# GpSimd's long elementwise operations issued in pieces of 256 elements a partition

## The chip, the cores and the metric

The kernel runs on one core of one Trainium2 chip. The metric is the device time of one execution, in microseconds (us). The kernel before takes 765.38 us, the median of 3 runs. The core's engines are TensorE (PE in the profile; PEld is its weight load), VectorE (DVE), ScalarE (ACT), GpSimd (POOL) and SyncE (SP, which issues most DMAs). Each works through its own instructions in order, and they meet at semaphores.

## The reference

Two transformer layers over x of 8 batches x 256 tokens x 256 channels, in float32. In each layer the attention and the feed-forward part read the same normalised input:

```python
xn = _layernorm(x)
x = x + _L0_attn_ref(xn, ...) + _L0_ffn_ref(xn, ...)
xn = _layernorm(x)
x = x + _L1_attn_ref(xn, ...) + _L1_ffn_ref(xn, ...)
```

- Layer 0 attention: 16 heads of 16 channels, causal, with a bias that is linear in the distance; the softmax's result is held to at least 1e-10.
- Layer 0 feed-forward: 8 experts, each `silu(xn @ Wg) * (xn @ Wu) @ Wd` with 256 hidden channels. All experts are computed, and their outputs are summed with routing weights.
- Layer 1 attention: 16 heads, causal, plain softmax.
- Layer 1 feed-forward: two linear layers (256 to 1024 to 256) with ternary weights, `alpha * sign(W) * (|W| > 0.05 max|W|)`, where alpha is the mean of the kept |W|; a gelu between them; and last a quantisation of the result to 4 bits with one scale for the whole tensor.

## The kernel before

**Numbers in two parts.** Most matmuls run on float16 pairs: a float32 tile is split into a high part (its float16 rounding) and a low part (the rest), and three products are summed (high by high, low by high, high by low). ScalarE makes the high part, and VectorE or GpSimd the low part by a subtraction. The weights of layer 0 (query/key, gate/up, down) are split once in the first pass: 14 tiles of 128 x 1024, of which GpSimd has the low parts of six (`POOL_SPLITS`, line 869) and VectorE the others. They come in through two alternating raw buffers, and the load of tile i + 2 waits until the low part of tile i is done.

**Experts.** For each batch and expert, TensorE makes `gate` and `up` (L1162), ScalarE a tanh and VectorE two operations that give the hidden tile `hid0` (128 x 512 float32). ScalarE writes its high part `h0_hi` (L1018), GpSimd its low part `h0_lo` (L880), and TensorE's `down` (L1173) needs both. Layer 1's hidden tile is eight blocks of 256; ScalarE writes the high parts of two blocks at a time (L1032), and GpSimd the low parts (L903).

**Ternary weights.** In the first pass, for W1 and then W2 (128 x 2048 float32 each): VectorE finds the largest |w|, and writes a tile of -1, 0 and 1. GpSimd multiplies the weights by it in place (L918), which leaves |w| where it is kept. ScalarE then makes two sums, of the kept |w| and of the squared signs (L958, L960). TensorE transposes the sums (step `tsm`, L1119) and VectorE makes alpha from them. Before its loop TensorE waits for both alphas (`pe.wait_ge(s_t, 2 * TERN)`).

**Attention.** For each head of layer 0: TensorE makes scores, VectorE adds the bias and takes the row maximum (L1555), ScalarE the exponential (L1037), VectorE the reciprocal of the sum (L1577) and the normalisation of the probabilities (L1580: one instruction of 256 and one of 128 elements, from SBUF to SBUF). TensorE then transposes them (L1233 to L1235). In layer 1 VectorE takes the maxima (L1569), and GpSimd masks the exponentials of the diagonal blocks (L889) before TensorE uses them (L1280).

**Order.** Batches are software pipelined: layer 1 of a batch runs beside layer 0 of the next. There are four kinds of pass: `first`, `steady` (a loop over 6 iterations), `last` and `final`. The order of the steps on each engine is written out by hand in `ORDER_TEXT`, once for each engine and kind. GpSimd's order in the loop is

```python
ln1a up up:1 h1 up:2 h1:2 h1:1 h1:3 up:3 up:4 mp +ln0a s:3 s mp:1 up:5 s:4 s:2 up:6 s:1 s:7 s:5
+xe s:6 up:7
```

where `up` is L880, `h1` L903, `s` L889, `ln0a` and `ln1a` the residual with its bias (L844) and the inverse deviation (L850). Nothing plans at run time: an engine that comes to a wait stands there.

Of the kernel before, what the change touches and what calls it, by code (L numbers as in the profile page):

```python
# [33 lines left out]
ALU = mybir.AluOpType  # L34
# [4 lines left out]
B, S, D = 8, 256, 256  # L39
H, C = 16, 16  # L40
NT = S // P
NK = D // P
E, F = 8, 256
NF = F // P
HID = 1024
# [300 lines left out]
def wait(eng, sem, value):  # L346

    if not (isinstance(value, int) and value <= 0):
        eng.wait_ge(sem, value)
# [21 lines left out]
def two_blocks(nc, x, wqk0, bqk0, wv0, vb0, wo0, ob0, slopes, wg, wu, wd, temp,  # L371
               wqk1, bqk1, wv1, vb1, wo1, ob1, w1t, b1c, w2t, b2, out):
    with ExitStack() as ctx:
        def sb(name, shape, dt=F32):
            return ctx.enter_context(nc.sbuf_tensor(name, shape, dt))

        def sem(name):
            return ctx.enter_context(nc.semaphore(name))
# [68 lines left out]
        hid0 = sb("hid0", [P, 2, NF, S])  # L447
        h0_hi = sb("h0_hi", [P, 2, NF, S], F16)
        h0_lo = sb("h0_lo", [P, 2, NF, S], F16)
        hid1 = sb("hid1", [P, NH, S])  # L450
        h1_parts = sb("h1_parts", [P, 2, NH, S], F16)
# [29 lines left out]
        raw = [v_sb[1][:].rearrange("p t b c -> p (t b c)")[:, 0:2 * NK * D], yx_sb[:].rearrange("p a t d -> p (a t d)")]  # L481
# [41 lines left out]
        s_lop = sem("s_lop")  # L523
        s_t = sem("s_t")
        s_tu = sem("s_tu")
# [27 lines left out]
        s_h0l = sem("s_h0l")  # L553
# [3 lines left out]
        s_h1l = sem("s_h1l")  # L557
# [37 lines left out]
        def split_parts(i):  # L595

            what, a = SPLIT[i]
            if what == "qk":
                return [w[a][:].rearrange("p k n -> p (k n)") for w in (qk_hi, qk_lo)]
            if what == "gu":  # L600
                return [w[:, a].rearrange("p m k f -> p (m k f)") for w in (gu_hi, gu_lo)]
            return [w[:, a:a + 2].rearrange("p e k d -> p (e k d)") for w in (wd_hi, wd_lo)]

        def his_done(i):
            return i + 1 + sum(k <= i for k in POOL_SPLITS)
# [6 lines left out]
        def tern_of(i):  # L612
            return ((w1_raw, t1_sb[:].rearrange("p k n -> p (k n)")), (w2_raw, t2_sb[:].rearrange("p a d -> p (a d)")))[i]
# [168 lines left out]
        def _(pool):  # L782
# [20 lines left out]
            def tables():  # L803

                pool.memset(ones[:], 0.0).then_inc(s_tab, 1)
                pool.memset(pieces[:], 0.0).then_inc(s_tab, 1)
                pool.memset(pick[:], 0.0).then_inc(s_tab, 1)
                pool.tensor_copy(ident_b[:], ident[:]).then_inc(s_tab, 1)
                pool.wait_ge(s_tab, 3)
                pool.memset(ones[:, C:2 * C], WSCALE).then_inc(s_tab, 1)  # L810

                for i, row in enumerate((0, 4, KR, KR + 4)):
                    if i:
                        pool.wait_ge(s_tab, 5 + i)
                    pool.affine_select(out=pick[:], in_=pick[:], compare_op=ALU.not_equal, fill=1.0, base=-row,
                                       pattern=[[-1, 4], [0, P]], channel_multiplier=1).then_inc(s_tab, 1)
# [13 lines left out]
            def do(st):  # L830
# [35 lines left out]
                if name == "split" and st.arg in POOL_SPLITS:  # L866
                    hi, lo = split_parts(st.arg)
                    pool.wait_ge(s_hi, his_done(st.arg))
                    pool.tensor_tensor(lo, raw[st.arg % 2], hi, ALU.subtract).then_inc(s_lop, 1)
                if name == "xe":  # L870
                    wait(pool, s_xl[0], n.at(1, 1))
                    wait(pool, s_h0, n.at(E))
# [4 lines left out]
                if name == "up":  # L877
                    e = st.arg % 2
                    wait(pool, s_h0h, n.at(E, st.arg + 1))
                    pool.tensor_tensor(h0_lo[:, e], hid0[:, e], h0_hi[:, e], ALU.subtract).then_inc(s_h0l, 1)  # L880
                if name == "s":
                    for hp in range(2):
                        s = 2 * st.arg + hp
# [16 lines left out]
                if name == "h1":  # L900
                    a = 2 * st.arg
                    wait(pool, s_h1h, n.at(NH // 2, st.arg + 1))
                    pool.tensor_tensor(h1_parts[:, 1, a:a + 2], hid1[:, a:a + 2], h1_parts[:, 0, a:a + 2],  # L903
                                       ALU.subtract).then_inc(s_h1l, 1)
                if name == "quant":
                    c = st.arg

# [6 lines left out]
                if name == "tern":  # L914
                    i, step = st.arg // TERN_STEPS, st.arg % TERN_STEPS
                    if step == 3:
                        pool.wait_ge(s_t, TERN * i + 6)
                        pool.tensor_tensor(tern_of(i)[0], tern_of(i)[0], tern_of(i)[1], ALU.mult).then_inc(s_tu, 1)  # L918
                    if i == 0 and step == 0:
                        tables()  # L920
                    if i == 1 and step == 5:
                        pool.wait_ge(s_lo, len(SPLIT) - len(POOL_SPLITS))
                        pool.wait_ge(s_lop, len(POOL_SPLITS))
                        pool.wait_ge(s_hi, his_done(len(SPLIT) - 1))
                        pool.memset(v_sb[1][:], 0.0).then_inc(s_v1z, 1)

            def before_block1():
                pool.sem_inc(s_h1l, NH // 2)
                pool.sem_inc(s_mp, 4)
                pool.sem_inc(s_mk, H)  # L930

            run_passes(nc, pool, do, before_block1, "gpsimd")


# [739 lines left out]
```

## Time and profile before

| | us |
|---|---|
| median of 3 runs | 765.38 (764.9 to 766.98) |
| the profiled execution | 762.38 |
| its span, first to last instruction | 760.6 |
| TensorE busy | 644.9 (85%), 6455 matmuls |
| VectorE busy | 570.8 (75%) |
| ScalarE busy | 465.4 (61%) |
| GpSimd busy | 270.1 (36%), 386 instructions |
| mean granted TensorE clock | 0.958 of full |

Durations below are from this one profiled execution. Busy time is what an engine spends in instructions, a wait not counted; it doesn't say which engine sets the end. For that there is the chain that ended last, which is followed back from the last instruction through whatever released each step. An instruction's duration on VectorE or GpSimd can contain time in which it stood, so the same shape with two durations is worth a look.

### The profile page before, as it was taken

How to read it: one execution, taken by the hardware profiler on the slowest of the kernel's cores; microseconds unless marked ns; L12 is line 12 of the kernel's file. 1: busy time of each engine (PE TensorE's matmuls, PEld its weight loads, DVE VectorE, ACT ScalarE, POOL GpSimd, SP SyncE). 2: the span in 40 equal slices, each digit the busy share in tenths (PEclk: the TensorE clock that was granted, in tenths of full speed). 3: DMA queues.
4: the chain of work that ended last, by engine and by line, in shares of the span. 5: the costliest groups of instructions: out<-in, count | busy, mean ns of one | idle time of the engine just before them, and what ended most of it. 6: DMA issues, size and time to landing. Idle time of an engine off the chain costs nothing.

```text
span 760.6 us, 19948 instructions
## 1 busy us (share of the span) xinstructions
PE 644.9 (85%) x6455; PEld 480.6 (63%) x6455; DVE 570.8 (75%) x2203; ACT 465.4 (61%) x1223; POOL 270.1 (36%) x386
## 2 busy tenths in 40 slices
PE   1476676989989997999889997999899997999773
PEld 0354554767666775777666775777676775767542
DVE  4489867796687948796779858796779768886557
ACT  2567765954379454965389445965398435963652
POOL 7846541224404241142404241233313331135336
PEclk9989998999999999999999999999999998999996
DMA  6843021300303030302212030302211030300453
GB/s 203 273 127 117 8 77 49 97 17 16 124 14 110 14 110 28 109 1 69 83 35 76 14 110 28 110 4 68 80 58 53 14 110 16 112 3 1 153 181 110
DMA packets 49555, 56.72 MB, mean 75 GB/s; under 512 B 5104, under 2 KB 40048, under 8 KB 49520
## 3 DMA queue, kind: packets, MB, share of 16 engines
q1 hardware_dynamic: 46480, 52.44, 21.6%
q0 software_dynamic: 1056, 2.62, 1.0%
q10 hardware_dynamic: 1984, 1.21, 0.5%
q8 instruction: 19, 0.31, 0.2%
q14 instruction: 16, 0.13, 0.1%
HBM read 33.71 MB, written 22.54 MB: 74 GB/s over the span
## 4 chain that ended last, share of the span: by engine, by line
PE 58%; DVE 16%; ACT 11%; issue 8%; POOL 2%; DMA 2%; ACTq 1%; SPq 1%; DVEq 1%; POOLq 0%
PE gen_ps L1162 16%; PE gen_ps L1173 9%; PE gen_ps L1135 6%; PE value_ps L1280 5%; PE gen_ps L1193 4%; PE gen_ps L1210 3%; ACT hid L1025 3%; PE value_ps L1286 3%; PE score_ps L1223 2%; ACT probs L1037 2%; DVE probs L1555 2%; DVE inv L1591 2%; DVE probs L1580 2%; PE turn_ps L1249 2%; PE turn_ps L1233 2%
## 5 line engine op out<-in xcount | busy, mean ns | idle before, releaser
L880 POOL TENSOR_TENSOR h_lo<-hid,h_hi 128x512 f16<-128x512 f32 x64 | 74.4, 1163 | 271.6 <-ACT h_hi L1018 271.6
L1037 ACT ACTIVATE probs<-probs,nmax 128x256 f32<-128x256 f32 (+1 forms) x256 | 113.4, 446 | 29.0 <-DVE nmax L1555 28.6
L1162 PE MATMUL gen_ps<-xe_hi,gu_hi 128*128 128x256 f16 x512 | 101.0, 280 | 2.1 <-issue 2.1
L1162 PE MATMUL gen_ps<-xe_lo,gu_hi 128*128 128x256 f16 x512 | 100.6, 279 | 0.0
L1162 PE MATMUL gen_ps<-xe_hi,gu_lo 128*128 128x256 f16 x512 | 100.4, 279 | 0.0
L1555 DVE CUSTOM_DVE_ANT_0 probs<-score_ps,bias 128x256 f32<-128x256 f32 (+1 forms) x256 | 79.1, 351 | 16.5 <-PE score_ps L1225 16.5
L1065 ACT ACTIVATE et<-turn_ps 128x384 f32<-128x384 f32 x124 | 54.0, 489 | 50.9 <-PE turn_ps L1255 48.6
L1569 DVE CUSTOM_DVE_ANT_0 junk<-score_ps,bias 128x256 bf16<-128x256 f32 x248 | 73.6, 353 | 14.2 <-PE score_ps L1225 13.3
L1580 DVE TENSOR_SCALAR probs<-probs,rsum 128x256 f32<-128x256 f32 (+1 forms) x256 | 76.5, 341 | 4.6
L1014 ACT ACTIVATE tanh_sb<-gen_ps 128x512 f32<-128x512 f32 x64 | 37.8, 591 | 64.6 <-PE gen_ps L1162 64.5
L889 POOL TENSOR_SCALAR_AFFINE_SELECT et<-et 128x256 f32<-128x256 f32 x128 | 51.3, 423 | 73.0 <-ACT et L1065 73.0
L1223 PE MATMUL score_ps<-k_stack,q_stack 64*128 64x256 f16 x252 | 36.3, 285 | 44.0 <-DVE nmax L1555 26.0
L1046 ACT ACTIVATE pt<-turn_ps 128x384 f32<-128x384 f32 x128 | 60.4, 482 | 20.3 <-PE turn_ps L1235 20.2
L1173 PE MATMUL gen_ps<-wd_hi,h_hi 128*128 128x256 f16 x256 | 50.1, 278 | 9.7 <-issue 6.8
L1223 PEld LDWEIGHTS score_ps<-k_stack,q_stack 64*128 64x128 f16 x252 | 12.2, 93 | 72.2 <-DVE nmax L1555 30.7
L1162 PEld LDWEIGHTS gen_ps<-xe_hi,gu_hi 128*128 128x128 f16 x512 | 47.7, 100 | 14.3 <-issue 8.4
L1162 PEld LDWEIGHTS gen_ps<-xe_lo,gu_hi 128*128 128x128 f16 x512 | 51.3, 100 | 7.0
L1513 DVE SCALAR_TENSOR_TENSOR acc<-gen_ps,w,acc 128x256 f32<-128x256 f32 x112 | 48.8, 477 | 9.2 <-PE gen_ps L1173 9.2
L1162 PEld LDWEIGHTS gen_ps<-xe_hi,gu_lo 128*128 128x128 f16 x512 | 51.2, 100 | 6.9
L1502 DVE SCALAR_TENSOR_TENSOR hid<-gated,gen_ps 128x512 f32<-128x512 f32 x64 | 43.8, 684 | 11.4 <-PE gen_ps L1162 10.7
L903 POOL TENSOR_TENSOR h_parts<-hid,h_parts 128x512 f16<-128x512 f32 x32 | 37.3, 1178 | 38.4 <-ACT h_parts L1032 38.4
L1497 DVE SCALAR_TENSOR_TENSOR gated<-tanh_sb,gen_ps 128x512 f32<-128x512 f32 x64 | 43.6, 682 | 9.7 <-ACT tanh_sb L1014 9.7
(225 smaller groups left out, 1662.7 us busy)
## 6 DMA issues: line engine op xcount, KB each, us to landing
scr_q<-parts SPq DMA_DIRECT2D x32, 256.0 KB, 2.7
scr_k<-parts SPq DMA_DIRECT2D x32, 256.0 KB, 3.0
q_stack<-scr_q SPq DMA_DIRECT2D x64, 128.0 KB, 3.0
k_stack<-scr_k SPq DMA_DIRECT2D x64, 128.0 KB, 3.1
x<-in_x SPq DMA_DIRECT2D x8, 256.0 KB, 2.7
y_dram<-yx_sb SPq DMA_DIRECT2D x7, 256.0 KB, 2.2
x_dram<-yx_sb SPq DMA_DIRECT2D x7, 256.0 KB, 2.2
out_dram<-gu_hi SPq DMA_DIRECT2D x7, 256.0 KB, 2.2
```

The costliest lines, as they stand in the source:

```text
L880: pool.tensor_tensor(h0_lo[:, e], hid0[:, e], h0_hi[:, e], ALU.subtract).then_inc(s_h0l, 1)
L889: pool.affine_select(out=on_diagonal, in_=on_diagonal, compare_op=ALU.is_ge, fill=0.0, base=0, pattern=[[0, NT], [1, P]], channel_multipli ...
L1037: last = act.activation(probs[:, k, lo:hi], probs[:, k, lo:hi], ACT.Exp, scale=-1.0, bias=nmax[:, k, j:j + 1], accum_out=esum[:, k, j:j + 1])
L1046: act.activation(pt[:, slot:slot + 3].rearrange("p t q -> p (t q)"), turn_ps[s % 2][:, 0:3 * P], ACT.Copy).then_inc(s_ev[0], 1)
L1065: act.activation(et[:, s % TURNED], pair_of(st)[hp][:, 0:3 * P], ACT.Exp).then_inc(s_ev[1], 1)
L1162: last = pe.matmul(g[:, S * f:S * f + S], w[:, st.arg, m, k, cols], xx[:, k, :], start=(i == 0), stop=(i == len(terms) - 1))
L1173: last = pe.matmul(g[:, D * t:D * t + D], h[:, st.arg % 2, f, P * t:P * t + P], w[:, st.arg, f, :], start=(i == 0), stop=(i == len(terms) ...
L1223: pe.matmul(pair[hp][:, 0:S], q[rows[hp], i, P:S], k[rows[hp], i, :], start=True, stop=True)
L1513: dve.scalar_tensor_tensor(acc[:, t], g[:, D * t:D * t + D], w8[:, t, e:e + 1], (xb[0] if st.place == 0 else acc)[:, t], ALU.mult, ALU.add)\
L1555: last = dve.tensor_tensor_reduce(out=probs[:, k, lo:hi], in0=g[:, lo:hi], in1=bias0[:, s, blo:S], scale=-1.0, scalar=BIG, op0=ALU.add, op ...
L1569: last = dve.tensor_tensor_reduce(out=junk[:, hp, lo:hi], in0=pair_of(st)[hp][:, lo:hi], in1=bias1[:, blo:S], scale=-1.0, scalar=BIG, op0= ...
L1580: last = dve.tensor_scalar(probs[:, k, lo:hi], probs[:, k, lo:hi], rsum[:, k, j:j + 1], CLAMP, ALU.mult, ALU.max)
```

## The change

Each of four kinds of GpSimd operation is issued as a row of instructions over 256 elements a partition, and the last one of them raises the semaphore that the one instruction raised before. The low parts of a weight tile (1024 elements) become four, those of a hidden tile (512, both layers) two, and a ternary product (2048) eight. Operands, types and the order of the steps stay as they were, and no other operation is touched.

```diff
--- before.py
+++ after.py
@@ -866,7 +866,9 @@
                 if name == "split" and st.arg in POOL_SPLITS:
                     hi, lo = split_parts(st.arg)
                     pool.wait_ge(s_hi, his_done(st.arg))
-                    pool.tensor_tensor(lo, raw[st.arg % 2], hi, ALU.subtract).then_inc(s_lop, 1)
+                    for c in range(0, 2 * NK * D, D):
+                        last = pool.tensor_tensor(lo[:, c:c + D], raw[st.arg % 2][:, c:c + D], hi[:, c:c + D], ALU.subtract)
+                    last.then_inc(s_lop, 1)
                 if name == "xe":
                     wait(pool, s_xl[0], n.at(1, 1))
                     wait(pool, s_h0, n.at(E))
@@ -877,7 +879,9 @@
                 if name == "up":
                     e = st.arg % 2
                     wait(pool, s_h0h, n.at(E, st.arg + 1))
-                    pool.tensor_tensor(h0_lo[:, e], hid0[:, e], h0_hi[:, e], ALU.subtract).then_inc(s_h0l, 1)
+                    for f in range(NF):
+                        last = pool.tensor_tensor(h0_lo[:, e, f], hid0[:, e, f], h0_hi[:, e, f], ALU.subtract)
+                    last.then_inc(s_h0l, 1)
                 if name == "s":
                     for hp in range(2):
                         s = 2 * st.arg + hp
@@ -900,8 +904,9 @@
                 if name == "h1":
                     a = 2 * st.arg
                     wait(pool, s_h1h, n.at(NH // 2, st.arg + 1))
-                    pool.tensor_tensor(h1_parts[:, 1, a:a + 2], hid1[:, a:a + 2], h1_parts[:, 0, a:a + 2],
-                                       ALU.subtract).then_inc(s_h1l, 1)
+                    for j in range(a, a + 2):
+                        last = pool.tensor_tensor(h1_parts[:, 1, j], hid1[:, j], h1_parts[:, 0, j], ALU.subtract)
+                    last.then_inc(s_h1l, 1)
                 if name == "quant":
                     c = st.arg
 
@@ -915,7 +920,10 @@
                     i, step = st.arg // TERN_STEPS, st.arg % TERN_STEPS
                     if step == 3:
                         pool.wait_ge(s_t, TERN * i + 6)
-                        pool.tensor_tensor(tern_of(i)[0], tern_of(i)[0], tern_of(i)[1], ALU.mult).then_inc(s_tu, 1)
+                        w, t = tern_of(i)
+                        for c in range(0, NK * HID, D):
+                            last = pool.tensor_tensor(w[:, c:c + D], w[:, c:c + D], t[:, c:c + D], ALU.mult)
+                        last.then_inc(s_tu, 1)
                     if i == 0 and step == 0:
                         tables()
                     if i == 1 and step == 5:
```

## Rows read from the trace of the kernel before

**Rows 1.** The page: busy time of TensorE, and the chain by engine.
```profile
PE 644.9 (85%) x6455; PEld 480.6 (63%) x6455; DVE 570.8 (75%) x2203; ACT 465.4 (61%) x1223; POOL 270.1 (36%) x386
PE 58%; DVE 16%; ACT 11%; issue 8%; POOL 2%; DMA 2%; ACTq 1%; SPq 1%; DVEq 1%; POOLq 0%
```

**Rows 2.** Waits, whole span: who waited for whom: us, times, longest.
```profile
PE gen_ps L1119 <- ACT hid L960: 5.8, 1, 5.8
...
PE gen_ps L1173 <- POOL h_lo L880: 0.2, 1, 0.2
```

**Rows 3.** GpSimd's groups by shape: count | busy us, mean ns | idle before.
```profile
L880 POOL TENSOR_TENSOR h_lo<-hid,h_hi 128x512 f16<-128x512 f32 x64 | 74.4, 1163 | 271.6 <-ACT h_hi L1018 271.6
...
L869 POOL TENSOR_TENSOR gu_lo<-yx_sb,gu_hi 128x1024 f16<-128x1024 f32 x3 | 6.4, 2130 | 3.1 <-ACT yx_sb L967 3.1
...
L918 POOL TENSOR_TENSOR hid<-hid,t_sb 128x2048 f32<-128x2048 f32 x1 | 4.1, 4077 | 4.1 <-DVE t_sb L1355 4.1
```

**Rows 4.** Timeline, GpSimd, 555 to 762: start, length, instruction; x2 is two merged.
```profile
577.37 2.28 POOL L903 TENSOR_TENSOR h_parts<-hid,h_parts 128x512 f16<-128x512 f32 x2 [0.61 <-ACT h_parts L1032]
...
592.19 1.41 POOL L844 TENSOR_TENSOR xb<-x,ob_sb 128x256 f32<-128x256 f32 x2
```

**Rows 5.** Chain that ended last, 72 to 125: start, length, what.
```profile
78.52 4.09 POOL hid L918
...
104.79 5.11 POOL h_parts L918
...
116.59 2.56 PE gen_ps L1162 x12
```

**Rows 6.** Timeline, VectorE, at 104.7.
```profile
104.73 1.22 DVE L1407 TENSOR_TENSOR parts<-rest,parts 128x1024 f16<-128x1024 f32 x1
```

**Rows 7.** Timeline, all engines, 244.8 to 246.5 (second loop iteration, expert 3).
```profile
244.92 1.17 POOL L880 TENSOR_TENSOR h_lo<-hid,h_hi 128x512 f16<-128x512 f32 x1 [0.65 <-ACT h_hi L1018]
...
246.21 0.39 PE L1173 MATMUL gen_ps<-wd_hi,h_hi 128*128 128x256 f16 x2
```

**Rows 8.** Timeline, all engines, 47 to 49.2 (first pass, expert 1).
```profile
47.47 1.32 POOL L880 TENSOR_TENSOR h_lo<-hid,h_hi 128x512 f16<-128x512 f32 x1 [5.55 <-ACT h_hi L1018]
...
48.89 0.58 PE L1173 MATMUL gen_ps<-wd_hi,h_hi 128*128 128x256 f16 x2 [3.34 <-issue]
```

**Rows 9.** Line L1580: duration in ns, least / median / most.
```profile
L1580 DVE TENSOR_SCALAR probs<-probs,rsum x256: 272/352/1185, 41.8 to 673.6; 128x256 f32<-128x256 f32 x128
```

**Rows 10.** Timeline, VectorE, 146 to 156 (first loop iteration).
```profile
146.93 1.45 DVE L1580 TENSOR_SCALAR probs<-probs,rsum 128x256 f32<-128x256 f32 x2
...
151.46 1.45 DVE L1580 TENSOR_SCALAR probs<-probs,rsum 128x256 f32<-128x256 f32 x2
...
153.80 0.84 DVE L1580 TENSOR_SCALAR probs<-probs,rsum 128x256 f32<-128x256 f32 x1
...
154.56 1.17 DVE L1580 TENSOR_SCALAR probs<-probs,rsum 128x128 f32<-128x128 f32 x1
```

**Rows 11.** Timeline, GpSimd, the same stretch.
```profile
147.10 1.20 POOL L903 TENSOR_TENSOR h_parts<-hid,h_parts 128x512 f16<-128x512 f32 x1 [2.94 <-ACT h_parts L1032]
...
151.57 1.26 POOL L903 TENSOR_TENSOR h_parts<-hid,h_parts 128x512 f16<-128x512 f32 x1 [0.61 <-ACT h_parts L1032]
153.34 2.31 POOL L903 TENSOR_TENSOR h_parts<-hid,h_parts 128x512 f16<-128x512 f32 x2 [0.51 <-ACT h_parts L1032]
```

**Rows 12.** Windows: stretch, length, busy (count) by engine, granted clock, DMA share, GB/s.
```profile
142.98:161.50 18.52, 14.86 (x137) 10.33 (x136) 16.19 (x62) 14.52 (x43) 8.26 (x7) 0.91 0.25 80
231.72:246.21 14.49, 13.46 (x137) 9.46 (x136) 12.80 (x60) 14.21 (x43) 8.17 (x7) 1.00 0.31 99
```

**Rows 13.** Timeline, VectorE, 233.5 to 236.9 (second loop iteration).
```profile
235.51 0.55 DVE L1580 TENSOR_SCALAR probs<-probs,rsum 128x256 f32<-128x256 f32 x2
```

**Rows 14.** Timeline, GpSimd, the same stretch.
```profile
235.83 1.24 POOL L903 TENSOR_TENSOR h_parts<-hid,h_parts 128x512 f16<-128x512 f32 x1 [2.94 <-ACT h_parts L1032]
```

## The prediction

> **What bounds the kernel now.** I read the page first: TensorE is busy 85% of the span and the chain that ended last runs 58% on TensorE, 16% on VectorE and only 2% on GpSimd [rows 1]. GpSimd has 270 us of work in 761, and the low parts of the experts' hidden tile alone have 271.6 us of idle time in front of them, waiting for ScalarE [rows 3]. So GpSimd is not the bound, and time added to it costs something only where another engine waits for its result within a fraction of a microsecond. The reader is to look for two things: those places, and places where a long GpSimd instruction holds up VectorE.
>
> **What one cut costs.** The change issues the same elements in pieces of 256 a partition: 64 and 32 tiles of 512 become two pieces, 6 tiles of 1024 four, 2 tiles of 2048 eight. That is 64 + 32 + 18 + 14 = 128 more instructions. By shape [rows 3], 512 elements take 1163 ns and 1024 take 2130 ns, so 1.889 ns an element and 196 ns fixed; this gives 4.06 us for 2048, and the row says 4.077. A piece of 256 is then 680 ns. Two back-to-back instructions overlap a little: two tiles of 512 take 2.28 us [rows 4], 0.15 us more than one of 1024. I take 0.15 us for a cut. The other nearest row is the bias sum, two instructions of 256 in 1.41 us [rows 4], 0.705 us each; eight of those make 5.64 us where the product takes 4.08, so 0.22 us a cut. Below, nothing excludes that the fixed part vanishes behind the piece before it: 0. All cuts together are 128 x 0.15 = 19 us of GpSimd time, nearly all of it in its idle time.
>
> The Trainium skill (GPSIMD Engine Reference, "Instruction dispatch") puts the dispatch of an instruction at an indirect call, tens of cycles. At its 1.2 GHz that is an estimate of 0.02 to 0.08 us a cut, where our rows show 0.15. By the page the two ternary products below would cost 0.3 to 1.1 us together, not 2.1; the trace decides, and I keep 0.15.
>
> **Ternary products (on the path, slower).** In the first pass the chain goes through both [rows 5]: product of W1 at 78.52 for 4.09 us, ScalarE's two sums behind it, then TensorE's transpose of the sums, for which TensorE sits idle 5.8 us [rows 2]. The product of W2 is at 104.79 for 5.11 us, its sums are transposed in the same way, and the first instruction of the loop on TensorE is at 116.59, as TensorE waits there for alpha. Seven cuts each: 2 x 7 x 0.15 = +2.1 us (bounds 0 and 3.1). The second product takes 1.03 us longer than the first because VectorE's subtraction with two SBUF inputs began at 104.73 [rows 6]; only its first piece waits for that, so that part stays. Nothing hides this term: TensorE, in order, stands at the transposes.
>
> **Low parts of the hidden tile, h_lo (64).** Each ends 0.15 us later. In the loop, TensorE's down product of expert 3 starts 0.13 us after its h_lo ends (244.92 + 1.17 to 246.21) [rows 7]. That is just a semaphore's way, so it moves by up to 0.15; I take 0.13 in five of six iterations, 0.65 us in all. In the first pass down product 1 starts at 48.89, right behind the h_lo that ends at 48.79, after 3.34 us of idling [rows 8]: +0.15. TensorE's waits name h_lo just once more, in the last pass [rows 2]: +0.15. Elsewhere matrix work of other steps stands between the two and is the cover. The h_lo behind the second ternary product is late with it, but TensorE then stands at the transpose anyway. Together 0.95 us, bounds 0 and 1.5 (seven times 0.22).
>
> **Low parts of the second hidden tile (32) and of the weights (6).** No wait of TensorE names the tile; its product comes behind the other steps of the iteration, which cover a few tenths. The weights' low parts end 3 x 0.15 = 0.45 us later each. They gate later loads and the gate products of the first pass, where nothing in the chain waits for GpSimd's part of them. Zero; if that cover is thin, 0.45 once or twice.
>
> **What the change gives back.** VectorE's normalisation of the probabilities (L1580, SBUF to SBUF) has a median of 352 ns and a maximum of 1185 [rows 9]. In the first iteration of the loop four of them, in three pairs, take 1.45, 1.45 and (0.84 + 1.17) us [rows 10] where a clear pair takes 0.55 [rows 13]; and each time a low part of the second hidden tile is running, from 147.10, 151.57 and 153.34 on [rows 11]. The lost time is 0.90 + 0.90 + 0.49 + 0.89 = 3.2 us. The same stretch of work, from the h_lo of expert 1 to the down product of expert 3, takes 18.52 us in this iteration and 14.49 in the next [rows 12], so 4.03 us are lost, part of it to TensorE's clock: 0.91 granted against 1.00, and the same 137 matmuls are busy 14.86 us against 13.46. With 1.4 us put down to that, 2.6 are left for the blocking.
>
> With pieces: the second norm of the pair at 146.93 (it begins 0.27 later) waits for the first piece only, which ends at 147.78; it is done near 147.87, not at 148.38. VectorE is then 0.5 us ahead, so the pair of 151.46 starts near 150.96 and is done before the low part of 151.57 starts. The third pair meets the second piece of the one before, at most. I take back 2.2 of the 2.6 us. Bounds: 0 (each norm then meets the next piece) and 4.0 (the clock of that stretch comes back as well). In iterations 2 to 6 nothing is blocked before: the pair at 235.51 [rows 13] has its second norm at 235.78 and the low part starts at 235.83 [rows 14]. There is nothing to gain there, and 0.05 us of margin.
>
> That the long instruction holds VectorE off until it ends agrees with the Trainium skill (SBUF — State Buffer, the exclusive lock of the shared port pair). Its other half speaks against the change: the one that starts first has the ports for its whole instruction, so each piece has to win them anew, and VectorE's long two-input operations can get in between. What that would cost here is the second rival below.
>
> **Sum.** +2.1 (ternary) +0.95 (h_lo) +0 (others) -2.2 (first iteration) = +0.85 us. On the profiled execution (762.38 us, span 760.6 and 1.8 around it) that is 763.2. That execution was 3.0 us quicker than the median of the runs, and the clock at which TensorE gets through an iteration differs from one to the next. The difference is carried to the median: 765.38 + 0.85 = 766.2 us. Its own range is 764.3 to 767.7.
>
> **Rivals.**
> 1. The blocking is not recovered: +3.05, 768.4 us, slower. Norms come in pairs. If the first gets in at a cut and the second meets the next piece, the pair ends when the tile ends, as before. For it: two of the three pairs last until the tile's end. Against: the norm begun at 153.80 is done at 154.64, between two low parts that run until 155.65, so VectorE does get in at a cut [rows 10, 11]. It decides once less than 0.75 us comes back, since 3.05 - 0.75 is 0.3% (2.3 us, about what a measurement can tell from no change).
> 2. Pieces lose the ports: new waits in the loop. Place: the pair at 235.51 and its likes, five iterations. Since the margin is 0.05 us, a slip of VectorE by 0.1 against ScalarE makes the second norm meet a piece of 0.68 us, and a loop iteration 0.4 to 0.6 us longer. 5 x 0.5 = 2.5 us on the forecast: 768.7. Against: the norms follow ScalarE's exponentials and the low parts follow ScalarE's copies, in a fixed order on one engine, so both slip together.
> 3. Faster: cuts cost a third of what I say (0.05 us, so +1.0 in all) and the first iteration gets back the whole 4.0: -3.0, 762.4 us. For it: no low clock in that stretch in the second iteration. Against: the fit of three sizes.
> 4. No piece gets VectorE in and nothing else waits: the change does only its cuts; this is rival 1 in time.
>
> **Chances.** Forecast 0.53, rivals 1 and 4 together 0.2, rival 2 0.1, rival 3 0.17. Range 762.5 to 769.1: from rival 3's edge to beyond rivals 1 and 2, which leaves out the upper bound of the cuts with no gain (765.38 + 3.1 + 1.5 = 770.0) and the lower bound of all. Faster by over 0.3% 0.17, within 0.3% 0.53, slower 0.3.
>
> **What would show it.** A piece of 256 near 680 ns, two pieces 1.31 us from start to end; the ternary products 5.1 and 6.2 us; the loop's first TensorE instruction 2 to 2.5 us later than 116.59. The stretch of the first iteration near 16 us, with no pair of norms over 1 us. Iterations 2 to 6 within 0.2 us of before at the same clock. The prediction is wrong in kind if norms in iterations 2 to 6 take over 0.6 us, or if TensorE waits for h_lo in other places than the three named.

## The result, and the profile after

| | before | after |
|---|---|---|
| median, us | 764.54 (761.84 to 766.98, 20 runs) | 767.62 (763.62 to 769.88, 20 runs) |
| profiled execution's span, us | 760.6 | 767.1 |
| GpSimd busy, us | 270.1, 386 instructions | 287.1, 514 instructions |
| mean granted TensorE clock | 0.958 | 0.947 |

The kernel became slower by 0.4%: the ratio is 1.0039, 95% interval [1.0026, 1.0052], which is +3.0 us [2.0, 4.0]. The forecast was +0.85 us, 766.2 us; the range 762.5 to 769.1 holds the result, but the likeliest case, a change under 0.3%, misses it by a little. The medians of more runs stand here; the 765.38 of the forecast was the median of the first three. The profiled execution of the kernel after was the slowest of its 20, 769.88 us.

First the page of the kernel after: busy time, then the chain by engine (before: [rows 1]).

```profile
PE 651.8 (85%) x6455; PEld 483.6 (63%) x6455; DVE 572.1 (75%) x2203; ACT 465.3 (61%) x1223; POOL 287.1 (37%) x514
...
PE 58%; DVE 16%; ACT 11%; issue 8%; DMA 2%; ACTq 1%; POOL 1%; SPq 1%; DVEq 1%; POOLq 0%
```

GpSimd's groups by shape (count | busy us, mean ns | idle before), which answer to [rows 3]:

```profile
L883 POOL TENSOR_TENSOR h_lo<-hid,h_hi 128x256 f16<-128x256 f32 x128 | 83.4, 673 | 265.2 <-ACT h_hi L1026 265.2
...
L908 POOL TENSOR_TENSOR h_parts<-hid,h_parts 128x256 f16<-128x256 f32 x64 | 41.8, 681 | 35.6 <-ACT h_parts L1040 35.6
...
L870 POOL TENSOR_TENSOR gu_lo<-yx_sb,gu_hi 128x256 f16<-128x256 f32 x12 | 7.8, 676 | 3.9 <-ACT yx_sb L975 3.9
```

A piece takes 673 to 681 ns. GpSimd has 17.0 us more work in 128 more instructions, 0.13 us each. The chain still hardly touches it. So the page says only that GpSimd did more, and not where three microseconds went. For that the timeline has to be read at places, the two ternary products first (GpSimd, start, length; before: [rows 5]):

```profile
83.04 5.07 POOL L925 TENSOR_TENSOR hid<-hid,t_sb 128x256 f32<-128x256 f32 x8 [4.80 <-DVE t_sb L1363]
...
110.64 6.08 POOL L925 TENSOR_TENSOR h_parts<-h_parts,t_sb 128x256 f32<-128x256 f32 x8 [8.84 <-DVE t_sb L1363]
```

They are 0.98 and 0.97 us longer. Then the first loop iteration. These are the windows of the same two stretches as in [rows 12], from the same TensorE instruction to the same one (length, busy by engine, granted clock, DMA share, GB/s):

```profile
149.82:164.53 14.71, 13.52 (x138) 9.49 (x136) 13.30 (x61) 14.37 (x43) 9.12 (x14) 1.00 0.31 100
234.72:249.43 14.71, 13.52 (x137) 9.47 (x136) 13.19 (x61) 14.37 (x43) 9.17 (x14) 1.00 0.32 98
```

The first iteration's stretch fell from 18.52 to 14.71 us and is now equal to the second's. The second's rose from 14.49 to 14.71. In the first iteration VectorE's normalisations stand so (before: [rows 10]), and GpSimd's low parts of the second hidden tile beside them (before: [rows 11]):

```profile
153.79 0.96 DVE L1588 TENSOR_SCALAR probs<-probs,rsum 128x256 f32<-128x256 f32 x2
...
157.82 0.55 DVE L1588 TENSOR_SCALAR probs<-probs,rsum 128x256 f32<-128x256 f32 x2
...
159.37 0.61 DVE L1588 TENSOR_SCALAR probs<-probs,rsum 128x256 f32<-128x256 f32 x2
```
```profile
153.95 1.35 POOL L908 TENSOR_TENSOR h_parts<-hid,h_parts 128x256 f16<-128x256 f32 x2 [2.80 <-ACT h_parts L1040]
...
158.34 1.30 POOL L908 TENSOR_TENSOR h_parts<-hid,h_parts 128x256 f16<-128x256 f32 x2 [0.47 <-ACT h_parts L1040]
160.11 2.56 POOL L908 TENSOR_TENSOR h_parts<-hid,h_parts 128x256 f16<-128x256 f32 x4 [0.47 <-ACT h_parts L1040]
```

Of the first pair, the first normalisation starts 0.16 us before the tile and isn't held; the second is let in after the first piece (the pair takes 0.96 us, where it took 1.45). The two pairs behind it come before their low part starts. So the kernel gains 3.8 us here, and must lose nearly 7 elsewhere. Where both kernels' TensorE instructions are set side by side in order, the one after is 6.84 us behind at the loop's first instruction:

```profile
123.43 0.61 PE L1170 MATMUL gen_ps<-xe_hi,gu_hi 128*128 128x256 f16 x2 [2.16 <-issue]
```

It stood at 116.59 [rows 5]. The first pass is where the loss is, and the ternary products are 2 us of it. One place more is in sight there. On VectorE and on GpSimd at 76 us:

```profile
76.28 1.40 DVE L1588 TENSOR_SCALAR probs<-probs,rsum 128x256 f32<-128x256 f32 x2
```
```profile
74.38 2.55 POOL L870 TENSOR_TENSOR wd_lo<-yx_sb,wd_hi 128x256 f16<-128x256 f32 x4 [4.53 <-ACT yx_sb L975]
```

A pair of normalisations that took 0.55 us at 72.65 in the kernel before now takes 1.40, beside a weight tile's low part that ends 0.42 us later than it did (2.55 for 2.13 us). Here each of the two normalisations is held by a GpSimd instruction of its own: the first (0.80 us for 0.35) by the tile's last piece, the second (0.69 for 0.28) by the first piece of the h_lo that follows without a gap. The prediction had put the weights' low parts at zero.

**A caution on single profiles.** The difference of the spans is 6.5 us, that of the medians 3.1. In a profile TensorE's clock drops at places that aren't the same in every execution. From 253.58 to 304.86 in the kernel before, and the same instructions after:

```profile
253.58:304.86 51.28, 46.78 (x515) 35.23 (x512) 37.70 (x145) 25.60 (x66) 17.50 (x33) 1.00 0.18 56
```
```profile
256.80:309.76 52.96, 48.45 (x516) 36.12 (x513) 38.92 (x151) 25.77 (x67) 18.17 (x38) 0.97 0.17 54
```

1.7 us are lost at a clock of 0.97. Nine of the twelve kernels below show the same step of 1.67 or 1.68 us, e1 and e4 among them, which change nothing in this stretch; e5, e6 and e12 don't. The other such place is the stretch with which the loop opens. In the kernel before, after and e2, from the loop's first TensorE instruction to the same later one:

```profile
116.59:133.09 16.50, 12.74 (x89) 8.88 (x90) 13.22 (x72) 9.68 (x31) 2.31 (x3) 0.79 0.08 26
```
```profile
123.43:139.95 16.52, 12.76 (x89) 8.87 (x90) 13.24 (x72) 9.67 (x31) 2.44 (x4) 0.80 0.05 17
```
```profile
117.93:132.63 14.70, 12.07 (x89) 8.63 (x90) 12.06 (x66) 9.61 (x30) 2.32 (x3) 0.77 0.10 29
```

It takes 16.5 to 16.6 us in the kernel before, the whole change, e9 and e12, and 14.1 to 15.0 us in the ten others. e9 and e1, one on either side, differ in no instruction of it, and with one profile of each kernel it stays open whether that difference of some 2 us belongs to the kernel or to the execution. It matters wherever a part is compared with the whole. So below, a place is judged by one stretch of a trace with its cause in view, and an amount by the ratio of medians.

### The profile page after: what moved, and what is told of

Same layout as the page of the kernel before. It is cut to its first block, busy times and chain, and to the rows that moved or that the text cites. A ratio compares the mean times of both kernels' runs of the same rounds, so it can differ in the third digit from the quotient of the medians.

```text
span 767.1 us, 20076 instructions
## 1 busy us (share of the span) xinstructions
PE 651.8 (85%) x6455; PEld 483.6 (63%) x6455; DVE 572.1 (75%) x2203; ACT 465.3 (61%) x1223; POOL 287.1 (37%) x514
## 4 chain that ended last, share of the span: by engine, by line
PE 58%; DVE 16%; ACT 11%; issue 8%; DMA 2%; ACTq 1%; POOL 1%; SPq 1%; DVEq 1%; POOLq 0%
PE gen_ps L1170 15%; PE gen_ps L1181 9%; PE gen_ps L1143 6%; PE value_ps L1288 5%; PE gen_ps L1201 4%; PE gen_ps L1218 3%; ACT hid L1033 3%; PE value_ps L1294 2%; ACT probs L1045 2%; PE score_ps L1231 2%; DVE probs L1563 2%; DVE inv L1599 2%; DVE probs L1588 2%; PE turn_ps L1241 2%; PE turn_ps L1257 2%
## 5 line engine op out<-in xcount | busy, mean ns | idle before, releaser
L883 POOL TENSOR_TENSOR h_lo<-hid,h_hi 128x256 f16<-128x256 f32 x128 | 83.4, 673 | 265.2 <-ACT h_hi L1026 265.2
L1181 PE MATMUL gen_ps<-wd_hi,h_hi 128*128 128x256 f16 x256 | 50.5, 280 | 11.2 <-issue 7.3
L908 POOL TENSOR_TENSOR h_parts<-hid,h_parts 128x256 f16<-128x256 f32 x64 | 41.8, 681 | 35.6 <-ACT h_parts L1040 35.6
```

Of the source, the lines that this page charges most:

```text
L883: last = pool.tensor_tensor(h0_lo[:, e, f], hid0[:, e, f], h0_hi[:, e, f], ALU.subtract)
L1181: last = pe.matmul(g[:, D * t:D * t + D], h[:, st.arg % 2, f, P * t:P * t + P], w[:, st.arg, f, :], start=(i == 0), stop=(i == len(terms) ...
```

## The experiments

Ratios are to the kernel before, run beside each on the same chip in five rounds; microseconds are worked out from the ratio times 764.5. They need not equal the difference of the two medians (for e2, which has six runs, -5.4 by the ratio and -4.5 by the medians).

**One part each: e1 to e4.** Each kernel is the one before with one hunk of the change and no other. Of each hunk the loop stands here, cut to one line; the last piece raises the semaphore as in the change.

```diff
e1: + for c in range(0, NK * HID, D): last = pool.tensor_tensor(w[:, c:c + D], w[:, c:c + D], t[:, c:c + D], ALU.mult)
e2: + for j in range(a, a + 2): last = pool.tensor_tensor(h1_parts[:, 1, j], hid1[:, j], h1_parts[:, 0, j], ALU.subtract)
e3: + for f in range(NF): last = pool.tensor_tensor(h0_lo[:, e, f], hid0[:, e, f], h0_hi[:, e, f], ALU.subtract)
e4: + for c in range(0, 2 * NK * D, D): last = pool.tensor_tensor(lo[:, c:c + D], raw[st.arg % 2][:, c:c + D], hi[:, c:c + D], ALU.subtract)
```

e1, ternary products. 

> Only the two ternary products are cut, into eight pieces each. Theory A (a cut costs 0.14 us of GpSimd time, and only the ternary products are on the path): 2 x 7 x 0.14 = +2.0 us against the kernel before; products of 5.1 and 6.1 us. Theory B (the first pass loses its time at the weights' low parts, which hold up loads and norms): +0.5 us or less, since a product's end is not what TensorE waits for last. Theory C (pieces lose the ports to VectorE in the loop): 0, as no piece of this kernel runs in the loop.

e2, second hidden tile. 

> Only the low parts of layer 1's hidden tile (32) are cut in two. Theory A: the two or three pairs of norms that stand behind a low part in the first loop iteration get free, -2 to -4 us, with the stretch from expert 1's low part to expert 3's down product at 14.5 to 16 us instead of 18.5. Theory B: 0, nothing of the first pass is touched. Theory C: new waits of 0.4 to 0.6 us in each of iterations 2 to 6, +2 us or more.

e3, experts' h_lo. 

> Only the low parts of layer 0's hidden tile (64) are cut in two. Theory A: +0.95 us, 0.13 in each of five loop iterations at the down product of expert 3, and 0.15 at two places outside. Theory B: +0.3 us, from the first pass only. Theory C: +2 us and norms over 0.6 us in iterations 2 to 6.

e4, weights' low parts. 

> Only the low parts of the six weight tiles of GpSimd are cut in four. Theory A: within 0.3 us of the kernel before; they end 0.43 us later each, and other work covers that. Theory B: +2 us or more, all of it before the loop's first TensorE instruction. Theory C: 0.

| part cut | median, us | ratio [95%] | us |
|---|---|---|---|
| e1 ternary products | 767.36 | 1.0037 [1.0012, 1.0062] | +2.8 [0.9, 4.7] |
| e2 second hidden tile | 760.15 | 0.9929 [0.9905, 0.9954] | -5.4 [-7.3, -3.5] |
| e3 experts' h_lo | 764.54 | 1.0003 [0.9981, 1.0024] | +0.2 [-1.5, +1.8] |
| e4 weights' low parts | 767.15 | 1.0040 [1.0022, 1.0057] | +3.1 [1.7, 4.4] |

The change is several changes of opposite sign: e2 is clearly faster, e1 and e4 are clearly slower, and e3 isn't told from no change. e1 confirms the ternary term: the TensorE instructions behind the two products are each 1.05 and 0.99 us later. e3's h_lo costs 0.13 us at the one place per iteration that was named; its down product starts 1.43 us behind h_lo's start (243.97, 1.30 long, to 245.40) where it was 1.29 before [rows 7]:

```profile
243.97 1.30 POOL L881 TENSOR_TENSOR h_lo<-hid,h_hi 128x256 f16<-128x256 f32 x2 [0.65 <-ACT h_hi L1020]
...
245.40 0.39 PE L1175 MATMUL gen_ps<-wd_hi,h_hi 128*128 128x256 f16 x2
```

e4 was the surprise: it costs as much as the ternary products. e2 is faster than the kernel before by 0.7%, more than the forecast's 2.2 us, and its interval holds the forecast's upper bound of 4.0; the trace shows 3.96 us in this stretch. Its windows, first and second iteration:

```profile
142.50:157.06 14.56, 13.45 (x137) 9.48 (x136) 13.18 (x60) 14.22 (x43) 8.70 (x11) 1.00 0.34 104
226.96:241.53 14.57, 13.45 (x137) 9.49 (x136) 13.01 (x60) 14.23 (x43) 8.74 (x11) 1.00 0.30 99
```

The granted clock of the first is 1.00 where it was 0.91, and the 137 matmuls are busy 13.45 us where they took 14.86. The 1.4 us that the prediction left as the clock's own came back with the blocking.

**Is it the early release? e5 and e6.** The same count of cuts at another place: the first piece short or the last.

```diff
-                    pool.tensor_tensor(h1_parts[:, 1, a:a + 2], hid1[:, a:a + 2], h1_parts[:, 0, a:a + 2],
-                                       ALU.subtract).then_inc(s_h1l, 1)
+                    lo, full, hi = (x.rearrange("p j s -> p (j s)") for x in
+                                    (h1_parts[:, 1, a:a + 2], hid1[:, a:a + 2], h1_parts[:, 0, a:a + 2]))
+                    for c, d in ((0, 64), (64, 512)):      # e5;  e6: ((0, 448), (448, 512))
+                        last = pool.tensor_tensor(lo[:, c:d], full[:, c:d], hi[:, c:d], ALU.subtract)
+                    last.then_inc(s_h1l, 1)
```

e5, 64 and 448. 

> Only the low parts of layer 1's hidden tile are cut, into 64 and then 448 elements. Theory A (a norm that came just behind the start of a low part is let in at the first cut): the cut comes after 0.3 us, the norms are free even earlier than with two halves, and the stretch from 148.8 to 161.5 of the kernel before is some 3.9 us shorter; -4 us against before. Rival D (the gain comes from more instructions or from a later end of the low part, wherever the cut is): the same -4 us here.

e6, 448 and 64. 

> The same cut at the other end: 448 and then 64 elements. Theory A: the first piece holds the norm for 1.03 us and not 0.65, so the gain goes: 0 to -1 us, and the norms that stand behind a low part in the first loop iteration take 1.0 to 1.2 us still. Rival D: -4 us, as with the cut at 64.

e5: 760.0 us, ratio 0.9952 [0.9931, 0.9973], -3.7 us. e6: 762.9 us, ratio 0.9990 [0.9967, 1.0014], -0.8 us. VectorE's three pairs in the first iteration, first of e5, then of e6:

```profile
147.50 0.60 DVE L1583 TENSOR_SCALAR probs<-probs,rsum 128x256 f32<-128x256 f32 x2
...
151.32 0.56 DVE L1583 TENSOR_SCALAR probs<-probs,rsum 128x256 f32<-128x256 f32 x2
...
153.09 0.61 DVE L1583 TENSOR_SCALAR probs<-probs,rsum 128x256 f32<-128x256 f32 x2
```
```profile
147.10 1.33 DVE L1583 TENSOR_SCALAR probs<-probs,rsum 128x256 f32<-128x256 f32 x2
...
151.51 1.33 DVE L1583 TENSOR_SCALAR probs<-probs,rsum 128x256 f32<-128x256 f32 x2
...
153.73 1.13 DVE L1583 TENSOR_SCALAR probs<-probs,rsum 128x256 f32<-128x256 f32 x2
```

With e6's low parts beside the first two of those:

```profile
147.27 1.35 POOL L906 TENSOR_TENSOR h_parts<-hid,h_parts 128x448 f16<-128x448 f32 x2 [2.95 <-ACT h_parts L1035]
...
151.66 1.36 POOL L906 TENSOR_TENSOR h_parts<-hid,h_parts 128x448 f16<-128x448 f32 x2 [0.60 <-ACT h_parts L1035]
```

Both tiles take 1.35 us in all, as two equal pieces do, so the length isn't it. A pair that begins 0.16 or 0.17 us before its tile is held, in its second normalisation, until the first piece ends: 0.60 us with 64 elements, 1.33 with 448. It is the place of the first cut that counts, since only the second normalisation meets the tile. Where the first one is held too, the second can meet the next GpSimd instruction, as at 76.28 in the whole change. The stretch of e6 took 17.36 us, and its clock was still down:

```profile
143.13:160.49 17.36, 14.72 (x137) 10.36 (x136) 15.45 (x63) 14.76 (x45) 8.79 (x11) 0.91 0.28 87
```

So the low clock goes with the blocking: over this stretch it is 0.91 in the kernel before and in all six kernels in which the pairs are held (e1, e3, e4, e6, e7, e9), and 1.00 in the whole change and in all six in which they are let in (e2, e5, e8, e10, e11, e12). In the kernel before, the granted clock was 1.00 until 157.8, behind the three held pairs, and 0.50 (1.2 of 2.4 GHz) from there to 161.2.

**Which weight tile? e7.** Only tile 11 of the 14 (down weights of experts 4 and 5) in four pieces.

```diff
+                    size = D if st.arg == 11 else 2 * NK * D
+                    for c in range(0, 2 * NK * D, size):
+                        last = pool.tensor_tensor(lo[:, c:c + size], raw[st.arg % 2][:, c:c + size], hi[:, c:c + size], ALU.subtract)
```

> Only one tile is cut in four: the low part of the down weights of experts 4 and 5, the fifth of GpSimd's six. Theory A2 (the loss of the cut weight tiles comes from this one, which ends 0.43 us later, right where the next hidden tile's low part begins, so that a pair of norms is held until the end of that): +1.3 to +1.6 us, with a norm over 1.1 us near 74 us. Rival E (the six tiles lose evenly, through their loads): +0.4 us, and no new long norm.

766.2 us, ratio 1.0029 [1.0012, 1.0045], +2.2 us. GpSimd and VectorE there, in e7:

```profile
71.01 2.56 POOL L871 TENSOR_TENSOR wd_lo<-yx_sb,wd_hi 128x256 f16<-128x256 f32 x4 [4.24 <-ACT yx_sb L970]
73.62 1.16 POOL L883 TENSOR_TENSOR h_lo<-hid,h_hi 128x512 f16<-128x512 f32 x1
```
```profile
72.99 1.87 DVE L1583 TENSOR_SCALAR probs<-probs,rsum 128x256 f32<-128x256 f32 x2
```

and TensorE, which waits for the next row maximum from VectorE. The instruction before the change, then in e7:

```profile
74.36 0.28 PE L1223 MATMUL score_ps<-k_stack,q_stack 64*128 64x256 f16 x2 [1.55 <-DVE nmax L1555]
```
```profile
76.03 0.39 PE L1226 MATMUL score_ps<-k_stack,q_stack 64*128 64x256 f16 x2 [2.87 <-DVE nmax L1558]
```

Before, the tile ended at 72.80 and h_lo began at 73.28; the pair of normalisations began at 72.65, was 0.55 us long and went through that gap. Three cuts add 0.43 us, the gap closes, and the first normalisation waits for the last piece and the second for all of h_lo: 1.32 us from a delay of 0.43. TensorE's wait is longer by the same 1.32. In the whole change h_lo is cut too and the pair takes 1.40 us.

The weights' tile before that one (gate and up weights) has a like place. In the kernel before, a pair of normalisations of the first pass, and GpSimd beside it:

```profile
61.33 1.34 DVE probs L1580 x2
```
```profile
60.36 1.16 POOL L880 TENSOR_TENSOR h_lo<-hid,h_hi 128x512 f16<-128x512 f32 x1
...
61.78 0.53 POOL L807 MEMSET pick<- 128x512 bf16 x1
```

The first normalisation of the pair takes 1.12 us there, and 1.53 to 1.56 in the four kernels in which that tile is cut (e4, e8, e12, the whole change), as the h_lo behind the tile ends 0.4 us later against it. TensorE's instructions behind it are 0.4 to 0.5 us later in these four, and not in e7. That is half of what e4 costs more than e7 (0.9 us, intervals overlapping). The two places make 1.8 of e4's 3.1 us; the rest is put to no place. The place also limits what is said of a cut: this normalisation isn't let in where h_lo ends (61.52), nor between the memsets that follow, but ends at 62.45, behind the third of them (61.78 + 0.53). Let in at the first boundary is shown for the cut low parts, not for every row of GpSimd instructions.

**Sums of parts: e8, e10, e12.** e8 is the whole change without the ternary cuts, e10 the second hidden tile and h_lo, e12 the whole change without h_lo's cuts; the hunks are those above.

> The whole change without the ternary products. Theory A with the four single results: +2.5 (weights) -4.5 (second hidden tile) +0 (first hidden tile) = -2 us. Rival F (the parts do not add: the gain in the first loop iteration needs the phase of the first pass as it was): 0 to +2 us.

> Both hidden tiles' low parts cut in two, weights and ternary products whole. Theory A: the gain of the second tile (-4.2 us) less the 0.7 to 0.9 us of the first tile: -3.4 us. Rival C (pieces lose the ports to VectorE): -2 us or less in size.

> The whole change except the experts' h_lo, which stays one instruction of 512. This asks what h_lo's cuts cost in company: alone they cost nothing measurable (1.0003 [0.9981, 1.0024]), while second hidden tile plus h_lo gives 0.9983 where the second hidden tile alone gives 0.9929 and 0.9952. Theory A (small, by the traces: 0.13 to 0.15 us in each of five iterations and a little in the first pass, about 0.7 to 1 us in all): ratio near 1.003, about 766.6 where before is 764.5; TensorE's start of expert 3's down product in iterations 2 to 6 moves by 0.06 us and not by 0.20. Theory B (h_lo's cuts cost 2 to 3 us once the second hidden tile is cut too): ratio near 1.000 to 1.001, 764.5 to 765.5. Under both the first loop iteration's stretch is 3.8 us shorter than before, and the weights' and ternary parts are as in the whole change.

| parts cut | median, us | ratio [95%] | us |
|---|---|---|---|
| e8 all but ternary | 762.69 | 0.9987 [0.9968, 1.0005] | -1.0 [-2.4, +0.4] |
| e10 second hidden tile and h_lo | 762.32 | 0.9983 [0.9955, 1.0011] | -1.3 [-3.4, +0.8] |
| e12 all but h_lo | 765.33 | 1.0018 [1.0004, 1.0032] | +1.4 [0.3, 2.4] |

e8 (expected -2) falls short of its expectation inside its interval, and e10 (expected -3.4) has it at the very edge. Rival C of e10 gets its number (less than 2 us gained), but not its mechanism: the trace has the first iteration's gain in full (14.71 us for 18.52) and 0.2 us lost in each later one. The whole less e8 is 4.0 us for the ternary cuts, where e1 says 2.8 and the traces 2.0; of the two profiles' difference, 2.2 us lie in the stretch with which the loop opens (16.5 and 14.3). The whole less e12 is 1.6 for h_lo, where the traces give 0.7: expert 3's down product of each iteration is later by 0.06 us in e12 and by 0.20 with h_lo's cuts, 0.14 x 5. e12 falls between the theories of its expectation. The four single parts add up to +0.7 us (+2.4 if e5's -3.7 is taken for the same gain as e2's -5.4); measured are +3.0 [2.0, 4.0]. With four terms of 1.4 to 1.9 us uncertainty each this is no contradiction. Whether h_lo's cuts cost 0.7 us or up to 2 is left open.

**The price of a cut: e9.** Pieces of 64 elements for the ternary products, 32 each.

```diff
+                        for c in range(0, NK * HID, 64):
+                            last = pool.tensor_tensor(w[:, c:c + 64], w[:, c:c + 64], t[:, c:c + 64], ALU.mult)
```

> Only the ternary products are cut, into 32 pieces of 64 elements each, so 62 cuts and not 14. Theory A (0.14 us a cut, all of it on the path): the products take 4.08 + 31 x 0.14 = 8.4 us, and the kernel +8.7 us. Rival G (most of a product's end is covered, and the loss of the eight-piece version came from elsewhere): under +4 us.

776.58 us, ratio 1.0175 [1.0147, 1.0204], +13.4 us [11.2, 15.6]. The products:

```profile
78.97 8.67 POOL L920 TENSOR_TENSOR hid<-hid,t_sb 128x64 f32<-128x64 f32 x32 [4.08 <-DVE t_sb L1358]
...
110.44 9.49 POOL L920 TENSOR_TENSOR h_parts<-h_parts,t_sb 128x64 f32<-128x64 f32 x32 [8.98 <-DVE t_sb L1358]
```

31 cuts add 8.67 - 4.08 = 4.59 us, 0.148 us each, and 9.49 - 5.11 = 4.38, 0.141 each: the price holds for pieces four times shorter. TensorE behind them is 4.58 and 4.39 us later, so all of it is on the path. That is 9.0 us, and the medians say 13.4: what is lost beyond the products' own length is not explained by this trace, and e1 has the same excess in small (2.8 for 2.0, inside its interval). 2.2 us of what separates the profiles of e9 and e1 lie, once more, in the stretch with which the loop opens (16.6 and 14.4). The place and the price of a cut are shown; that they are the whole price isn't.

**Finer pieces: e11.** The second hidden tile's low parts in four pieces of 128.

```diff
...
+                    for c, d in ((0, 128), (128, 256), (256, 384), (384, 512)):
+                        last = pool.tensor_tensor(lo[:, c:d], full[:, c:d], hi[:, c:d], ALU.subtract)
```

> Only the second hidden tile's low parts are cut, in four pieces of 128 elements. Theory A: the norms are free after one cut already, so nothing more is gained; two more cuts (0.28 us) move the low part's end over the norm that starts there in iterations 2 to 6: -4 us, 0 to 0.5 us behind the halves. Rival D (each further cut frees VectorE further): -5 us or more.

762.37 us, ratio 0.9993 [0.9970, 1.0016]. A tile is now 1.64 us long for 1.35:

```profile
147.31 1.64 POOL L906 TENSOR_TENSOR h_parts<-hid,h_parts 128x128 f16<-128x128 f32 x4 [2.95 <-ACT h_parts L1035]
```

That is -0.5 us [-2.3, +1.2], where -4 was expected. The first iteration's gain is there in full (3.7 us in the stretch), but in each of the iterations 2 to 6 the same stretch is 0.30 us longer than before, as GpSimd comes to expert 3's h_lo later; with halves it is 0.05. The trace thus has 1.5 us of loss against 0.3, and the remaining 2 us or more between e11 and the halves are not explained. The release is had with the first cut; the trace shows each further one only paid for.

## Why the prediction was right in its range and low in its size

**Right.** A cut was put at 0.15 us: it is 0.14 in the change (5.07 - 4.08 over 7 cuts, 2.55 - 2.13 over 3), 0.148 in e9. A piece of 256 is 673 to 681 ns, for 680. The ternary products are on the path for their whole extra length, +2.0 us for +2.1. That the first iteration's normalisations are let in at the first cut, and that the second pair then comes before its tile, is what the rows after show, so rival 1 (a pair still ends with its tile) is out in the loop; e6, where it nearly does, is its control. The measured +3.0 us is nearly rival 1's +3.05, but that is chance: what rival 1 denies came back in full, and the loss came from elsewhere. Its mechanism, the first normalisation let in at a cut and the second held by the next piece, does occur at 76.28, where the prediction didn't look. Rival 2 is out in its size: in iterations 2 to 6 the stretch is 0.2 us longer, not 0.4 to 0.6, and no normalisation in them takes over 0.6 us (the longest is 0.52). h_lo's term was 0.13 us at expert 3, and 0.13 to 0.14 it is.

**Low: the give-back, -2.2 us for -3.8.** The step that failed is the split of 4.03 us into 2.6 for blocking and 1.4 for the clock, with the clock left as it was. In e2, e5 and the whole change the stretch runs at 1.00 and in e6, with the blocking, at 0.91. The clock followed the stalls; it was no second cause. The bound of 4.0 was the right value.

**Wrong: "Zero" for the weights' low parts, +3.1 us in e4.** The prediction looked for waits of TensorE for these tiles, found none, and stopped. The tile's own consumer indeed doesn't care. But the same holding of VectorE by GpSimd that the prediction counted as a gain in the loop works here as a loss: tile 11 runs into the gap through which VectorE's normalisations passed, and 0.43 us of GpSimd become 1.32 us of TensorE. The hedge (0.45 once or twice) took the delay itself for the price, and the price is what the delay makes VectorE wait for. At the tile before it, delay and price were about the same, 0.4 us.

The two errors, -1.6 and +3.1, turn +0.85 into +2.35. The 0.65 us that are left to +3.0 are less than the uncertainty of any one part. That the range held is partly luck, as the errors have opposite signs: with the weights' error alone the sum would have been +3.95, or 769.3 us, outside the range. The "what would show it" list caught this in part: the loop's first TensorE instruction was to be 2 to 2.5 us later, and it is 6.84 us later. Of that, 2.0 are the products, 0.9 the place at tile 11 and 0.5 the one at the tile before it. A further 1.8 us is lost between 37.80 and 48.89 (times of the kernel before), where h_lo's cut accounts for 0.15 at most. The kernels with one part show anything from -0.07 to +1.19 over the same instructions, e2 (+1.07) among them, which is unchanged there; so one profile can't say how much of it is the change's. The other 1.6 us are put to no place.

**What beats both kernels.** The second hidden tile alone, in two pieces: 760.15 us (e2) and, with the first cut after 64 elements, 760.0 us (e5); against the kernel before -0.7% and -0.5%. The intervals overlap, so which is better isn't known.

That VectorE is held until the GpSimd instruction ends, and not until the last of a row of them does, agrees with the Trainium skill (SBUF — State Buffer, "Who interferes with whom"), where whichever starts first has the shared pair of ports for the whole instruction: in the whole change the normalisation at 154 ends 0.1 us behind the first of its tile's two pieces. The tens of cycles of its GPSIMD Engine Reference ("Instruction dispatch") are the cost of finding and calling an instruction's code, one of the four stages that the page lists, and so no price of a cut. Taken for one, as the prediction's estimate of 0.02 to 0.08 us did, they are too low: the traces have 0.14 to 0.15 us a cut.

## What to carry to other kernels

Cut a long GpSimd instruction only where the trace shows another engine held until it ends, and put one cut early; each further cut is 0.14 us of GpSimd time, and on a serial path all of it is paid. When an engine's work gets longer by a few tenths, look not only at who waits for its result but at which two-engine conflict its new end runs into: the gap before its next instruction may be somebody's only way through. And a low clock inside a stalled stretch should be counted as coming back with the stall, until a trace shows otherwise.

## What was not expected of the hardware

- A VectorE instruction that is held by a GpSimd instruction is let in at the first cut, though the next piece follows without a gap: with pieces of 64 and 448 elements the pair of normalisations took 0.60 us, with 448 and 64 it took 1.33 us, for the same 1.35 us of GpSimd work. In a row of h_lo and three memsets it was let in only behind the third memset (61.33 in the kernel before).
- A small delay of GpSimd can cost three times its length: 0.43 us made 1.32 us (the pair at 72.99 in e7), since each of the two normalisations was held by a different GpSimd instruction, and the second by one that the pair had been ahead of.
- TensorE's granted clock stayed at 1.00 in the stretch where three pairs weren't held and was 0.91 where they were, with the same 137 matmuls: 13.45 us of busy time in e2 against 14.72 in e6.
